# A Mamba scan on one core: silu by ScalarE's own function, the D x term and the dt x copy on VectorE

## The reference

```
xz = h @ W_in;  xm, z = split(xz)
xm = silu(causal_conv4(xm) + conv_b)
dtr, B, C = split(xm @ W_xp)
dt = softplus(dtr @ W_dt + b_dt);  A = -exp(A_log)
for each step:  state = state * exp(dt * A) + (dt * xm) * B
                y = sum over n of state * C
y = (y + xm * D_param) * silu(z)
out = (y @ W_out) * gate
```

## Time and profile before

| what | us |
|---|---|
| median of 3 runs (2242.9 to 2256.2) | 2250.18 |
| the profiled execution, its own time | 2247.94 |
| its span in the profile | 2246.2 |
| busy: TensorE, VectorE, ScalarE, GpSimd | 1974.4, 1918.6, 1657.3, 1627.6 |

### The profile page before, as it was taken

The page is one execution under the profiler, slowest core; times in us unless marked ns, Lnnn a source line. Parts: engine busy times, 40 slices in busy tenths (PEclk is TensorE's granted clock), DMA queues, the critical chain, the costliest instruction groups (busy, mean ns, idle before and its releaser), DMA issues. The chain is left out here.

```text
span 2246.2 us, 44074 instructions
## 1 busy us (share of the span) xinstructions
PE 1974.4 (88%) x13241; PEld 1546.2 (69%) x13241; DVE 1918.6 (85%) x3655; ACT 1657.3 (74%) x3652; POOL 1627.6 (72%) x1864
## 2 busy tenths in 40 slices
PE   4899999995479999999999999999999999999870
PEld 3566666663157787877878787887878777787860
DVE  2788888885159999999999999999999999999983
ACT  0455555552379898988989898898988989898740
POOL 2799999995596786968778696776968678695320
PEclk8999999997789999999999999999999999999995
DMA  5122222211000000000000000000000000000308
GB/s 147 36 66 59 67 64 61 67 55 47 5 11 11 11 15 8 15 14 11 11 11 15 15 11 11 11 11 11 16 15 11 11 11 15 6 6 6 155 18 296
DMA packets 71549, 80.85 MB, mean 36 GB/s; under 512 B 12243, under 2 KB 63635, under 8 KB 69268
## 3 DMA queue, kind: packets, MB, share of 16 engines
q1 hardware_dynamic: 66132, 69.65, 9.8%
q10 hardware_dynamic: 5184, 8.39, 1.1%
HBM read 44.46 MB, written 33.55 MB: 35 GB/s over the span
## 5 line engine op out<-in xcount | busy, mean ns | idle before, releaser
L630 ACT ACTIVATE decay<-dtT,decay_rate 128x256 f32<-128x256 f32 x2048 | 870.0, 502 | 0.2
L513 PE MATMUL bank<-ident,decay 128*128 128x128 f32 x4096 | 624.1, 275 | 73.8 <-ACT decay L630 35.8
L523 PEld LDWEIGHTS bank<-ident,scaled 128*128 128x128 f32 x4096 | 494.4, 143 | 214.2 <-issue 191.4
L523 PE MATMUL bank<-ident,scaled 128*128 128x128 f32 x4096 | 623.6, 275 | 0.0
L513 PEld LDWEIGHTS bank<-ident,decay 128*128 128x128 f32 x4096 | 481.6, 142 | 92.5 <-ACT decay L630 82.9
L444 POOL TENSOR_SCALAR scaled<-state,bc 128x512 f32<-128x512 f32 x384 | 268.0, 706 | 215.6 <-DVE state L758 198.2
L444 POOL TENSOR_SCALAR scaled<-fresh,bc 128x512 f32<-128x512 f32 x384 | 276.1, 725 | 169.6 <-DVE fresh L758 93.2
L748 DVE TENSOR_TENSOR bank<-bank,state 128x512 f32<-128x512 f32 x512 | 342.6, 696 | 31.8 <-PE bank L513 28.6
L748 DVE TENSOR_TENSOR bank<-bank,fresh 128x512 f32<-128x512 f32 x512 | 342.0, 696 | 31.5 <-PE bank L513 27.3
L758 DVE SCALAR_TENSOR_TENSOR fresh<-dtx,bc,bank 128x512 f32<-128x512 f32 x512 | 358.4, 743 | 0.0
L758 DVE SCALAR_TENSOR_TENSOR state<-dtx,bc,bank 128x512 f32<-128x512 f32 x512 | 358.2, 743 | 0.0
(11 more groups left out here) (139 smaller groups left out, 3318.2 us busy)
## 6 DMA issues: line engine op xcount, KB each, us to landing
xt<-in_x_dram SPq DMA_DIRECT2D x64, 128.0 KB, 2.3
resid<-x SPq DMA_DIRECT2D x64, 128.0 KB, 1.8
normed<-xh SPq DMA_DIRECT2D x64, 128.0 KB, 1.7
xg<-normed SPq DMA_DIRECT2D x64, 128.0 KB, 2.1
ssm_out<-yo SPq DMA_DIRECT2D x32, 256.0 KB, 2.0
fin_r<-resid SPq DMA_DIRECT2D x8, 1024.0 KB, 13.0
mask_bc<-in_mask_BxS_ik_dram SPq DMA_DIRECT2D x64, 64.0 KB, 2.9
fin_y<-ssm_out SPq DMA_DIRECT2D x32, 128.0 KB, 2.9
```

The lines of the kernel that those rows point to most:

```text
L513: mm = pe.transpose(dec_bank[i % DECAY_BANKS][:, m * P:(m + 1) * P], decay[:, i // BLOCK % 2, n % GROUP, m, t % HALF * P:(t % HALF + 1) * ...
L523: mm = pe.matmul(y_bank[t % HALF][:, m * P:(m + 1) * P], scaled[:, i % RING, m * P:(m + 1) * P], ident[:, :], is_transpose=True, start=Fal ...
L630: act.activation(decay[:, block % 2, e // CB, m, :], dtT[c % 2][:, m, half * HTOK:(half + 1) * HTOK], ACT.Exp, scale=decay_rate[:, m, n:n ...
```

## The change

Silu of x and of z becomes ScalarE's Silu, each in one instruction of 128x2048 in place, both in slot 9: `silu_x` for the next chunk, after all 12 taps, and `silu_z` for the chunk being scanned. z's side banks are moved by a Copy, and `gate_x`, `gate_z` and `x_tanh` go. The skip term leaves TensorE: `seed` on VectorE writes D x into the y bank in slots 2, 6, 34 and 38, right behind the gate of the same bank, and waits for that gate. VectorE's `copy_x` takes over the copy of the turned dt x, in slots 58, 60, 3 and 6. The factors of 2 go from W_xp, D and mod_gate, and with them seven setup instructions; two setup products on TensorE open the y banks once. Slots are spread anew: dtr now in 13 and 14, z0 before dt0, u in 43 to 55, taps from 46, Ln in 36.

```diff
-        SLOTS = {"dtr": at(B1, 7, 14), "out1": at(B3, 9, 10, 11), "dt0": at(B1, 17), "z0": at(B1, 18, 19),
-                 "bcT": at(B1, 20, 21), "dt1": at(B1, 22), "bc": at(B1, 24, 25), "z1": at(B1, 26, 27),
-                 "dt2": at(B1, 28), "z2": at(B1, 30, 31), "dt3": at(B1, 32), "z3": at(B1, 34, 35),
-                 "h0": at(0, 37), "h1": at(0, 39), "u0": at(0, 41, 43), "u1": at(0, 45, 47), "u2": at(0, 49, 51),
-                 "u3": at(0, 53, 55), "out0": at(B2, 61, 62, 63),
+        SLOTS = {"dtr": at(B1, 13, 14), "out1": at(B3, 9, 10, 11), "dt0": at(B1, 18), "z0": at(B1, 16, 17),
+                 "bcT": at(B1, 20, 21), "dt1": at(B1, 23), "bc": at(B1, 24, 25), "z1": at(B1, 28, 29),
+                 "dt2": at(B1, 27), "z2": at(B1, 32, 33), "dt3": at(B1, 31), "z3": at(B1, 35, 36),
+                 "h0": at(0, 38), "h1": at(0, 39), "u0": at(0, 43, 44), "u1": at(0, 46, 48), "u2": at(0, 50, 52),
+                 "u3": at(0, 54, 55), "out0": at(B2, 60, 61, 63),
                  "x0": at(B1, 57), "x1": at(B1, 59), "x2": at(B2, 2), "x3": at(B2, 5)}
-        POOL_TAP_SLOTS = at(45, *range(2 * len(POOL_TAPS)))
-        X_ORDER, X_TANH, X_GATE = (0, 1, 2, 3), (57, 61, B1 + 3, B1 + 9), (59, 63, B1 + 5, B1 + 11)
-        MOVE_AFTER = {"dtr": 2, "bcT": 2, "z1": 2, "z2": 2, "z3": 2}
-        MODULATE, CARRY, LN = at(0, 14, 18), B1 + 9, B1 + 37
-        Z_GATES = at(B1, 20, 28, 32, 36)
+        POOL_TAP_SLOTS = at(46, *range(2 * len(POOL_TAPS)))
+        SILU = B1 + 9
+        MOVE_AFTER = {"dtr": 2, "bcT": 2}
+        X_COPY = tuple(SLOTS[f"x{t}"][0] + 1 for t in range(T))
+        MODULATE, CARRY, LN = at(0, 14, 18), B1 + 9, B1 + 36
...
             def sum_state(c, i):
                 n, t = item_of(i)
+                if n == 0:
+                    pe.wait_ge(s_skip, c * T + t + 1)
...
-            def skip_term(c, t):
-                if t == 0:
-                    pe.wait_ge(s_xs, (c + 1) * CB)
-                reached(pe, s_gated, c * T + t - HALF + 1)
-                for m in range(CB):
-                    mm = pe.matmul(y_bank[t % HALF][:, m * P:(m + 1) * P], d_diag[:, m, :],
-                                   xs[c % 2][:, m, t * P:(t + 1) * P], ...)
...
+            def silu_x(k):
+                act.wait_ge(s_tapadd, (k + 1) * len(POOL_TAPS))
+                x = xs[k % 2][:, :, :].rearrange("p a b -> p (a b)")
+                act.activation(x, x, ACT.Silu).then_inc(s_xs, 1)
+
+            def silu_z(k):
+                for b in range(CB):
+                    moved(act, k, f"z{b}")
+                z = zs[k % 2][:, :, :].rearrange("p a b -> p (a b)")
+                act.activation(z, z, ACT.Silu).then_inc(s_zs, 1)
...
+            def seed(c, t):
+                if t == 0:
+                    ve.wait_ge(s_xs, c + 1)
+                if c == 0:
+                    ve.wait_ge(s_pe, 4 + HALF)
+                reached(ve, s_gated, c * T + t - HALF + 1)
+                ve.tensor_tensor(y_bank[t % HALF][:, :].rearrange("p (a b) -> p a b", b=P),
+                                 xs[c % 2][:, :, t * P:(t + 1) * P], d_col[:, :, None].to_broadcast([P, CB, P]),
+                                 ALU.mult).then_inc(s_skip, 1)
...
+            def copy_x(k, t):
+                filled(ve, k, f"x{t}")
+                ve.tensor_copy(dtx[k % 2][:, t, :], side_of(k, f"x{t}")[:, :])\
+                    .then_inc(s_side_moved[side_turn(k, f"x{t}")[0]], 1)
```

More of the change, by code:

```diff
@@ L505, in mamba_tensor @@
             pe.wait_ge(s_prep, 1)
+            for y in y_bank:
+                pe.matmul(y[:, :], ident[:, :], w_in[:, 0, 0:512], start=True, stop=True).then_inc(s_pe, 1)
             def turn_decay(c, i):
@@ L567, in fill @@
                 elif kind == "dtr":
-                    pe.wait_ge(s_xs, k * CB + 2 * piece + 2)
+                    pe.wait_ge(s_xs, k + 1)
                     for g in range(P // DTR):
-                        m = X_ORDER[2 * piece + g]
+                        m = 2 * piece + g
                         mm = pe.matmul(side[g * DTR:(g + 1) * DTR, :], w_xp[:, m, 0:DTR], x[:, m, :],
@@ L591, in fill @@
                     mm.then_inc(s_side_filled, 1)
-            SKIPS = [index_of(0, t) + LAG - 1 for t in range(T)]
             def slot(c, i):
@@ L638, in move @@
                 if kind == "z":
-                    act.activation(zs[k % 2][:, b, :], side[:, :], ACT.Tanh, scale=0.5).then_inc(s_ztanh, 1)
-                    return
+                    ins = act.activation(zs[k % 2][:, b, :], side[:, :], ACT.Copy)
                 elif kind == "h":
@@ L655, in move @@
                     if b == 0:
-                        act.wait_ge(s_xs, (k + 1) * CB)
+                        reached(act, s_decay, (k - 1) * BLOCKS * GROUP * CB)
                     act.activation(dtT[k % 2][:, b, :], side[:, :], ACT.Relu, bias=dt_bias[:, b:b + 1])
                     ins = act.activation(tmp[:, b, :], side[:, :], ACT.Abs, bias=dt_bias[:, b:b + 1])
-                elif kind == "x":
-                    ins = act.activation(dtx[k % 2][:, b, :], side[:, :], ACT.Copy)
                 ins.then_inc(s_side_moved[side_turn(k, job)[0]], 1)
@@ L707, in slot @@
                     k = chunk_at(c, i, SLOTS[job][-1] + MOVE_AFTER.get(job, 1))
-                    if k is not None and job[:3] != "out":
+                    if k is not None and job[:3] != "out" and job[0] != "x":
                         move(k, job)
-                for step, position in enumerate(X_TANH):
-                    k = chunk_at(c, i, position)
+                for start, silu in ((SILU, silu_x), (SILU + B1, silu_z)):
+                    k = chunk_at(c, i, start)
                     if k is not None:
-                        x_tanh(k, step)
+                        silu(k)
                 k = chunk_at(c, i, LN)
@@ L763, in gate @@
                 if t == 0:
-                    for b in range(CB):
-                        moved(ve, c, f"z{b}")
+                    ve.wait_ge(s_zs, c + 1)
                 ve.wait_ge(s_summed, c * ITEMS + index_of(DS - 1, t) + 1)
@@ L780, in rows @@
                 ve.sem_inc(s_yo, 1)
-            def gate_z(k, b):
-                ve.wait_ge(s_ztanh, k * CB + b + 1)
-                side, z = side_turn(k, f"z{b}")[0], zs[k % 2][:, b, :]
-                ve.scalar_tensor_tensor(z, z, 1.0, side_bank[side][:, :], ALU.add, ALU.mult)\
-                    .then_inc(s_side_moved[side], 1)
-            def gate_x(k, step):
-                ve.wait_ge(s_xtanh, k * CB + step + 1)
-                x = xs[k % 2][:, X_ORDER[step], :]
-                ve.scalar_tensor_tensor(x, dtT[k % 2][:, X_ORDER[step], :], 1.0, x, ALU.add, ALU.mult)\
-                    .then_inc(s_xs, 1)
+            def copy_x(k, t):
+                filled(ve, k, f"x{t}")
+                ve.tensor_copy(dtx[k % 2][:, t, :], side_of(k, f"x{t}")[:, :])\
+                    .then_inc(s_side_moved[side_turn(k, f"x{t}")[0]], 1)
             def two_slots(c, i):
@@ L805, in two_slots @@
                         gate(c, t)
+                for t in range(T):
+                    if scanned(c) and i == index_of(0, t) + 2:
+                        seed(c, t)
                 if scanned(c):
@@ L809, in two_slots @@
                 for s in (i, i + 1):
+                    for t in range(T):
+                        k = chunk_at(c, s, X_COPY[t])
+                        if k is not None:
+                            copy_x(k, t)
                     for job in ROWS:
@@ L813, in two_slots @@
                             rows(k, job)
-                    for b, position in enumerate(Z_GATES):
-                        k = chunk_at(c, s, position)
-                        if k is not None:
-                            gate_z(k, b)
-                    for step, position in enumerate(X_GATE):
-                        k = chunk_at(c, s, position)
-                        if k is not None:
-                            gate_x(k, step)
             for c in BODIES:
```

26 lines of the change are left out of this document (3 added, 23 removed).

## The result

The kernel after takes 2228.82 us (median of 4 runs, 2225.83 to 2231.18). Beside it the kernel before took 2253.19 (4 runs, 2242.9 to 2257.47). The ratio is 0.9898, 95% interval 0.986 to 0.9936: faster by 1.0%. The profiled execution took 2225.83 us with a span of 2224.1, against 2247.9 and 2246.2.

What follows compares the result with a forecast made beforehand. VectorE was taken as nearest the bound, TensorE as the bound where fills crowd (slots 9 to 35). 13 x (-2.1) + 3.6 + 5.0 - 2.5 = -21 us from 2247.9 gives 2227, range 2205 to 2264.

Steps and rivals of the forecast that it cites:

- Steady chunk, 94.4 by arithmetic: Slots 0 to 63: VectorE to 15.2, TensorE's slots 9 to 32 to 52.5, VectorE to 63.1, then to 94.4 us.
- The Ln stall priced at nothing: Slots 40 to 45: stalls after the Ln cost nothing; if that cover were gone, 2 to 2.7 us come back.
- The allowance of 0.6: Steady chunk: 0.6 us added for late u fills and small delays, bounds 0 and 2.2, giving 95.0.
- The u fills, said to be late next: Slots 43 to 55: u fills cost TensorE 18.2 us against VectorE's 16.3, about what its lead covers.
- the second rival: Slots 2 and 6: gaps idle TensorE, its clock falls, 1.7 us lost; no change, about 2248 us, chance 0.25.
- Wait behind the gate 0.29, seed 0.65: VectorE, four times a chunk: gate costs 0.89 instead of 0.60 as the seed waits for it; seed itself 0.65 us.
- The copies, 0.60 each: VectorE: four added copies a chunk, PSUM to SBUF, 512 columns, each taken as 0.60 us like the gate.
- The silu block, covered by 0.1 us: ScalarE, slot 9: load, two silus, load, 6.4 us; decays reach TensorE's slots 15 to 17 in time, 0.1 us at narrowest.
- a chance of 0.19 on this block: Rival: silu block uncovered, slower, 2283 us with 4 us uncovered; chance 0.16, and another 0.03 for ScalarE table drains.
- The ends: Outside steady chunks: chunk 14 +3.6, last chunk +5.0, start -2.5 us with bounds -7 and +2.
- the signs that were named: Right if: chunks 94.5 to 95.5, gate-seed gap 0.2, waits some 4 us in slots 10 to 33, one load pair.
- the signs of being wrong: Decay waits in slots 15 to 17, several 1.2 GHz stretches per chunk, seeds over 0.9 us, four extra table loads.

Runs made afterwards that it cites:

- filler: The kernel after plus throw-away matmuls on TensorE at the ends of slots 3 and 7; 2213.44 us, 94.46 us a steady chunk.
- seed_plus2: The kernel after with the D x seeds two slots later (slots 4, 8, 36, 40), away from the gate; 2217.69 us.
- out_early: The kernel after with the three pieces of out1 in slots 7, 8, 9 instead of 9, 10, 11; 2200.09 us.
- copy_scalar: The kernel after with the four copies of the turned dt x back on ScalarE, seeds kept; 2225.49 us.
- silu_longer: The kernel after with two more silu of 2048 columns in ScalarE's block, between the silu of x and that of z; 2238.84 us.

## Why the prediction was right, and where its steps were not

The forecast was 2227, the median is 2228.8; the sum of changes was -21, the profiled executions differ by 2225.83 - 2247.9 = -22.1. The forecast came out this close in part by luck: several terms were wrong, and their errors cancel. By its steps:

- **Steady chunk, 94.4 by arithmetic.** The short chunks take 94.43. Within chunk 7 slots 0 to 7 took 1318.36 - 1303.00 = 15.36 (15.2 expected); TensorE started slot 9 at 15.2 (14.9) and took 37.6 for slots 9 to 32 (37.56); slots 40 to 63 took 31.4 (31.3). Between them TensorE's 0.4 us too many and the cheaper seeds of slots 34 and 38 cancel: slot 40 comes at 63.1, as worked out. The Ln stall priced at nothing is gone: every pair from slot 40 to 56 takes 2.51 us.
- **The allowance of 0.6.** It was 1.13 on average, by another cause than named. The u fills, said to be late next, cost nothing. The cost is the clock: 1.6 us in 9 of 13 chunks, 14.7 us in all, where 13 x 0.6 = 7.8 us were allowed for something else. That is the mechanism of the second rival, with its place (the gaps that gate and seed leave at slots 2 and 6) and nearly its price (1.3 to 1.7). It did not eat the gain, as its price was counted in full on top of the forecast and for all chunks: 13 x (95.56 - 95.0) = 7 us came over the forecast, not 18 to 24. filler, seed_plus2 and out_early show it from three sides.
- **Wait behind the gate 0.29, seed 0.65.** Both off. The seed starts 0.71 to 0.78 behind the gate, 0.11 to 0.18 later than the 0.60 of an instruction that need not wait; rows still takes 0.89 to 0.90. The seed takes 0.76 beside a busy GpSimd (slots 2 and 6) and 0.61 where it is quiet (slots 34 and 38). Together 1.47 to 1.55 in slots 2 and 6 and 1.33 in 34 and 38, against 1.54 for all four. The Trainium skill (VectorE: DVE Perf Modes, "The DRAIN you can't avoid") has the semaphore free; the gap behind the gate comes nearer to that than the one behind rows, and neither is nothing.
- **The copies, 0.60 each.** As measured (1310.67 to 1311.27). By copy_scalar they are no loss: without a fall of the clock they gain 0.6 us a chunk.
- **The silu block, covered by 0.1 us.** Covered, by 2.6 (silu_longer). The taps end at 16.1 us instead of 17.0, and the first load lies ahead of the wait, so the decays go on at 1324.17 - 1303.00 = 21.2 instead of 23.4, while TensorE comes to slot 15 at 26.3, 0.4 later than worked out. The load that runs ahead of the wait, left as an "if" in the prediction, is worth 1.3 us and should have been in the bounds. With it in the sum the margin would have been 1.4 us, and a chance of 0.19 on this block was too much. The page of the Trainium skill that it was weighed against (ScalarE: Activation LUTs, "What ACT_TABLE_LOAD costs") adds a drain of 1380 ns to each load; here too the load at 1322.87 ends at 1324.15 and the decays start at 1324.17.
- **The ends.** Chunk 14 +3.2 (3.6 expected), the last one 88.9 instead of 85.4, +3.5 (5.0; gates and seeds take 0.8 us less than priced). At the start -7.2 instead of -2.5, just past its bound of -7: the first chunk starts 12.7 us sooner (630.5 against 643.2) and then lasts 5.5 longer (99.3 against 93.8). I had both signs and neither size. The chunk starts while GpSimd is still at its taps: TensorE's sum waits 7.09 us for the first state that GpSimd scales, and ScalarE 8.30 us for the last tap (TensorE, then ScalarE, kernel after). By slot 8 the chunk is 6.6 us behind that of the kernel before. ScalarE's wait costs TensorE little: the longest wait for a decay just behind it is 0.50 us.

```profile
646.64 1.09 PE L525 MATMUL bank<-ident,scaled 128*128 128x128 f32 x4 [7.09 <-POOL scaled L442]
...
653.95 1.91 ACT L669 ACTIVATE xs<-xs 128x2048 f32<-128x2048 f32 x1 [8.30 <-POOL xs L458]
```

These misses and that of the allowance cancel: 13 x (-1.58) + 3.2 + 3.5 - 7.2 = -21.0; what comes behind the last chunk is another 0.9 us shorter.

Of the signs that were named, the single pair of loads around both silus is there, and VectorE's waits for TensorE are 3.2 us a chunk in slots 10 to 33 (before 1.4) and none in 40 to 45 (before 2.5). Two are missed: neither kind of chunk lies within 94.5 to 95.5 us, and the recorded gap between gate and seed is 0.03 to 0.10 us, not 0.2. Of the signs of being wrong none shows from chunk 1 on: no turn waits for decays in slots 15 to 17, and no seed takes over 0.9 us.

So the total is better than its parts. What the prediction did not say, and the runs do: the change is a gain of 3.6 us a chunk, of which its own pieces on VectorE give 2.1 back.

Open: why the same 2.04 us of idle time is followed by a fall of the clock in nine chunks of 13 and not in the others. In silu_longer the same gap of 2.04 us leaves 10 of 13 chunks without a fall, in copy_scalar one of 2.06 us leaves 9. What holds the three fastest kernels at 93.3 to 93.5 us a chunk is open too. And silu with the slots of before was not tried with dtr in slot 7.

## What to carry to other kernels

Look at what an added instruction stands in front of, not at how free its engine is: D x cost VectorE 3 us of work a chunk, but its price was set by the turn that waited behind it, and two slots later it was cheaper. Work that a second engine did in its own idle time is not a saving when it is moved, and may have kept that engine's clock up. When a sum comes out right, undo the parts one by one all the same: here one of them was worth 25 us the other way.

## What the hardware showed that I had not expected

- A table load executed ahead of the wait of the instruction that needs it: 1.28 us at 1316.23, while the taps that the silu of x waits for were done at 1319.1.
- Throw-away matmuls on TensorE shorten the run: 95.56 to 94.46 us a chunk.
- What it costs VectorE to wait for the result of the instruction in front is not one figure, for tiles of the same 512 columns. Over the 0.60 us without such a wait it is 0.11 where the seed has this one wait (slots 6, 34 and 38), 0.18 where it waits for x too (slot 2), and 0.29 behind rows, where a signal to the store stands between as well. In the first chunk the seeds of slots 34 and 38 have a second wait and also start 0.79 behind the gate. So it seems to grow with what stands between the two instructions.
